# List batches of 9, 9, 12 and 6 tiles, with their work spread over other iterations of the main loop

## What is computed

```python
q = x @ Wq.T + bq; k = key @ Wk.T + bk; v = value @ Wv.T + bv
scores = (q @ k.T) / sqrt(4096)
adj_scores = scores * adj
adj_scores = where(abs(adj_scores) < 1e-05, -1e9, adj_scores)
prob = softmax(adj_scores, axis=-1)
y = (prob @ v) @ Wm.T + bm
out = layernorm(x + y)
```

## Time and profile before

| | |
|---|---|
| median of 3 runs | 504.44 us (504.05 to 504.83) |
| the profiled execution | 507.02 us, span 505.2 us |
| granted TensorE clock, mean | 0.971 |
| PE busy | 455.5 us, 90% |
| VectorE (DVE) busy | 329.7 us, 65% |
| Pool (POOL) busy | 258.7 us, 51% |
| ScalarE (ACT) busy | 215.2 us, 43% |
| DMA | 119.73 MB, mean 237 GB/s |

### The profile page before, as it was taken

The page is one execution under the profiler, slowest core; times in us unless marked ns, Lnnn a source line. Parts: engine busy times, 40 slices in busy tenths (PEclk is TensorE's granted clock), DMA queues, the critical chain, the costliest instruction groups (busy, mean ns, idle before and its releaser), DMA issues.

```text
span 505.2 us, 5747 instructions
## 1 busy us (share of the span) xinstructions
PE 455.5 (90%) x1556; PEld 250.0 (49%) x1556; DVE 329.7 (65%) x905; ACT 215.2 (43%) x471; POOL 258.7 (51%) x258
## 2 busy tenths in 40 slices
PE   6999999999998398999998878589999989999981
PEld 2444444444443145665655545356666555665551
DVE  0155444599239914889899889976875864654774
ACT  1223322233331124434653444425656536556574
POOL 2100001201860017788787888617777757777730
PEclk9999999999999879999998999979999989999998
DMA  8999998799999958999999999818677665765743
GB/s 312 357 212 247 276 286 209 134 269 290 258 301 273 271 140 261 242 275 271 238 330 296 261 304 294 255 49 254 187 226 242 213 198 172 221 188 168 227 151 123
DMA packets 42037, 119.73 MB, mean 237 GB/s; under 512 B 7109, under 2 KB 11973, under 8 KB 40978
## 3 DMA queue, kind: packets, MB, share of 16 engines
q0 software_dynamic: 19008, 70.59, 56.6%
q1 hardware_dynamic: 15842, 28.91, 16.2%
q10 hardware_dynamic: 7152, 19.83, 10.7%
HBM read 140.61 MB, written 17.83 MB: 314 GB/s over the span
## 4 chain that ended last, share of the span: by engine, by line
PE 53%; DVE 30%; ACT 7%; issue 5%; DMA 4%; POOL 1%; DVEq 0%; POOLq 0%; ACTq 0%
PE bank L548 13%; PE bank L539 10%; PE bank L681 7%; PE bank L661 7%; PE bank L641 4%; DVE big L981 3%; PE bank L579 3%; DMA big<-adj_tiles 3%; PE bank L593 3%; DVE big L1020 3%; DVE big L1018 2%; DVE y_buf L1183 2%; DVE big L983 2%; DVE big L1051 2%; DVE big L1048 2%
## 5 line engine op out<-in xcount | busy, mean ns | idle before, releaser
L548 PE MATMUL bank<-big,M 128*128 128x456 f32 x288 | 121.6, 548 | 1.8 <-DMA big<-xT 1.8
L539 PE MATMUL bank<-y_buf,big 128*128 128x512 f32 x256 | 111.2, 594 | 0.0
L428 POOL DMA_INDIRECT key_g<-key,index x72 | 77.0, 1070 | 43.0 <-DVE index L1062 22.0
L439 POOL DMA_INDIRECT v_g<-table,index x72 | 78.4, 1089 | 36.5 <-issue 18.3
L450 POOL DMA_INDIRECT adj_g<-adj_cols,index x72 | 75.5, 1048 | 21.9 <-issue 21.6
L419 POOL DMA_DIRECT2D big<-adj_tiles x36 | 20.6, 574 | 122.5 <-PE bank L539 69.8
L981 DVE TENSOR_TENSOR big<-big 128x1824 bf16<-128x1824 bf16 x36 | 39.6, 1101 | 60.4 <-DMA big<-adj_tiles 60.4
L539 PEld LDWEIGHTS bank<-y_buf,big 128*128 128x128 f32 x256 | 48.2, 190 | 59.6 <-issue 59.6
L681 PE MATMUL bank<-v_g,probT 128*114 128x512 f32 x140 | 70.5, 628 | 0.0
L661 PE MATMUL bank<-keyT,qT 128*114 128x256 f32 x288 | 68.5, 381 | 0.8 <-ACT keyT L854 0.5
L548 PEld LDWEIGHTS bank<-big,M 128*128 128x128 f32 x288 | 49.6, 190 | 33.1 <-issue 33.1
(11 more groups left out here) (115 smaller groups left out, 535.6 us busy)
## 6 DMA issues: line engine op xcount, KB each, us to landing
big<-adj_tiles POOLq DMA_DIRECT2D x36, 912.0 KB, 11.0
x_buf<-x SPq DMA_DIRECT2D x36, 256.0 KB, 4.9
out<-y_buf SPq DMA_DIRECT2D x35, 256.0 KB, 2.7
big<-valueT ACTq DMA_DIRECT2D x8, 1024.0 KB, 11.4
big<-xT SPq DMA_DIRECT2D x7, 912.0 KB, 8.6
table<-qT ACTq DMA_DIRECT2D x5, 1024.0 KB, 20.1
table<-y_buf ACTq DMA_DIRECT2D x3, 1024.0 KB, 23.8
big<-xT ACTq DMA_DIRECT2D x2, 912.0 KB, 20.2
```

Of the source, the lines that this page charges most:

```text
L428: pool.indirect_dma_start(key_g[:, b, c, :], None, key, bass.IndirectOffsetOnAxis(index[:, t, c:c + 1], 0), bounds_check=N - 1, oob_is_err ...
L439: pool.indirect_dma_start(v_g[:, b, c, :], None, table, bass.IndirectOffsetOnAxis(index[:, t, c:c + 1], 0), bounds_check=N - 1, oob_is_err ...
L539: mm = nc.tensor.matmul(bank[4 + t % 2][:, :], col_buf[nb % 2][:, d, k * P:(k + 1) * P], G[:, d, :], start=(d == 0), stop=(d == DC - 1))
L548: mm = nc.tensor.matmul(ps[:, 0:QR], M[:, d, a * P:(a + 1) * P], col_buf[nb % 2][:, d, 0:QR], start=(d == 0), stop=(d == DC - 1))
```

## The change

The tiles are dealt to four batches of 9, 9, 12 and 6 (`BATCH`, `START`); the third has 96 cells, the fourth 48. The operands of the list work are cut to the batch's partitions; `cell_count` and `cell_need` are cleared at the start, since not every partition is written now.

Tiles 20 to 29 are reduced in iterations 0 to 9 and tiles 30 to 35 in 15 to 20. Pool's loads move with them (they follow `trees_of(i + 3)`). Batch 2 has its steps in iterations 10 to 15, batch 3 in 21 to 26. There are six steps instead of eight: step 0 has numbering, count and a pass, steps 1 and 2 two passes each, step 3 the last pass, the bits and the first two pairs of the shift, step 4 the other six pairs, step 5 the index. Numbering moves behind the weights and statistics, and `add_x` stays ahead of the weights in step 0 too. `COUNTS` goes from 25 to 27.

On PE the lists' products (`lists`, `sum_counts`, `spread_slots` and the two of the overflow test) move from behind the scores to just ahead of the transposes of the probabilities.

Ahead of the loop `value_sums` moves from behind tile 19 to between batch 1's last pass and its bits, and `index_slots(1)` behind `key_bias(0)`. Pool waits for an index at tiles 0, 9, 18 and 30 instead of 0, 9, 18 and 27.

The diff, cut to its core:

```diff
-BT = 9
-LB = T // BT
+BATCH = (9, 9, 12, 6)
+START = (0, 9, 18, 30)
+LB = len(BATCH)
+BT = max(BATCH)
...
-        TREES = [[t] for t in range(FIRST, T)]
-        LIST_AT = {2: 8, 3: 17}
-        COUNTS = 25
+        TREES = {i: [FIRST + i] for i in range(10)} | {i: [FIRST + i - 5] for i in range(15, 21)}
+        LIST_AT = {2: 10, 3: 21}
+        COUNTS = 27
...
-                if at <= i <= at + PASSES + 1:
+                if at <= i <= at + 5:
...
-                if t % BT == 0:
-                    pool.wait_ge(index_ready, (t // BT + 1) * (2 * CH))
+                if t in START:
+                    pool.wait_ge(index_ready, (START.index(t) + 1) * (2 * CH))
...
             def lists(b):
-                pe.wait_ge(any_sb, (b + 1) * BT)
+                n = BATCH[b] * G8
+                pe.wait_ge(any_sb, START[b] + BATCH[b])
                 if b > 2:
                     pe.wait_ge(index_ready, b * (2 * CH))
                 for k in range(K4):
-                    mm = nc.tensor.matmul(list_bank(b)[0:CELLS, k * P:(k + 1) * P],
-                                          any_[:, k, b * BT:(b + 1) * BT, :].rearrange("p t g -> p (t g)"),
+                    mm = nc.tensor.matmul(list_bank(b)[0:n, k * P:(k + 1) * P],
+                                          any_[:, k, START[b]:START[b] + BATCH[b], :].rearrange("p t g -> p (t g)"),
                                           ident16[:, :], start=True, stop=True)
                 mm.then_inc(list_ps, 1)
...
-                if step == 0:
-                    lists(b)
-                if step == 1:
-                    sum_counts(b)
-                if step == PASSES + 1:
-                    spread_slots(b)
-                if i == COUNTS + 1:
-                    pe.wait_ge(lead_sb, 2)
-                    for k in range(2):
-                        mm = nc.tensor.matmul(bank[6][0:1, k * P:k * P + CELLS], lead[:, k:k + 1], ident[0:CELLS, 0:CELLS],
-                                              start=True, stop=True)
-                    mm.then_inc(lead_ps, 1)
                 if i >= 1:
                     values(i - 1)
                 if i + 1 < T:
@@ -718,6 +711,18 @@
                     if i == 0:
                         pe.wait_ge(bits_sb, 2 * 2)
                     project(u, bank[7], 0, 1)
+                if step == 0:
+                    lists(b)
+                if step == 1:
+                    sum_counts(b)
+                if step == 5:
+                    spread_slots(b)
+                if i == COUNTS + 1:
+                    pe.wait_ge(lead_sb, 2)
+                    for k in range(2):
+                        mm = nc.tensor.matmul(bank[6][0:1, k * P:k * P + CELLS], lead[:, k:k + 1], ident[0:CELLS, 0:CELLS],
+                                              start=True, stop=True)
+                    mm.then_inc(lead_ps, 1)
...
+            nc.vector.memset(cell_count[:, :], 0.0).then_inc(filled, 1)
+            nc.vector.memset(cell_need[:, :], 0.0).then_inc(filled, 1)
...
-            def shift_lists(b):
-
+            def shift_lists(b, first, last):
+
+                c = cells_of(b)
                 dve.wait_ge(took, (b + 1) * (2 * PASSES))
-                wide = LIST
-                for k in range(SHIFTS):
+                for k in range(first, last):
                     by = 1 << k
+                    wide = min(LIST + by - 1, ROOM)
...
-                if t == 2 * BT - 1:
+                if t == START[2] - 1:
                     number(1)
                     count(1)
                     for k in range(PASSES):
                         take_8(1, k)
+                    value_sums()
                     shift_bits(1)
-                    shift_lists(1)
-            value_sums()
-            index_slots(1)
+                    shift_lists(1, 0, SHIFTS)
             dve.wait_ge(prep_sb, 2 * DC + 2)
             key_bias(0)
+            index_slots(1)
...
-                if step == 0:
-                    number(b)
-                elif 1 <= i <= LAST_QUERY:
+                if 1 <= i <= LAST_QUERY:
                     add_x(i - 1)
                 if i < T:
                     weigh(i)
-                if i >= 1 and (step == 0 or i > LAST_QUERY):
+                if i > LAST_QUERY:
                     add_x(i - 1)
                 if 1 <= i < T:
                     statistics(i - 1)
                 if i == T:
                     last_statistics(T - 1)
-                if step == PASSES + 1:
+                if step == 5:
                     index_slots(b)
                 for t in trees_of(i):
                     reduce_tile(t)
                 if step == 0:
+                    number(b)
                     count(b)
-                if step is not None and step < PASSES:
-                    take_8(b, step)
-                if step == PASSES:
+                    take_8(b, 0)
+                if step in (1, 2):
+                    take_8(b, 2 * step - 1)
+                    take_8(b, 2 * step)
+                if step == 3:
+                    take_8(b, PASSES - 1)
                     shift_bits(b)
-                    shift_lists(b)
+                    shift_lists(b, 0, 2)
+                if step == 4:
+                    shift_lists(b, 2, SHIFTS)
```

More of the change, by code:

```diff
@@ L1004, in count @@
                     dve.wait_ge(took, b * (2 * PASSES))
-                nc.vector.tensor_scalar(lw, left[:, b, :], 0.0, 0.0, ALU.is_gt, ALU.add,
-                                        accum_out=cell_count[:, b:b + 1]).then_inc(counted, 1)
+                nc.vector.tensor_scalar(lw[c, :], left[c, b, :], 0.0, 0.0, ALU.is_gt, ALU.add,
+                                        accum_out=cell_count[c, b:b + 1]).then_inc(counted, 1)
                 for k in range(2):
-                    nc.vector.memset(dense[k], 0.0).then_inc(cleared, 1)
+                    nc.vector.memset(dense[k][c, :], 0.0).then_inc(cleared, 1)
                 dve.wait_ge(counted, b + 1)
@@ L1012, in take_8 @@
             def take_8(b, i):
+                c = cells_of(b)
                 k = b * (2 * PASSES) + 2 * i
-                src = left[:, b, :] if i == 0 else lw
+                src = left[c, b, :] if i == 0 else lw[c, :]
                 if i:
                     dve.wait_ge(took, k)
-                row = dense[0][:, 8 * i:8 * i + 8]
+                row = dense[0][c, 8 * i:8 * i + 8]
                 nc.vector.max(row, src).then_inc(took, 1)
                 dve.wait_ge(took, k + 1)
-                nc.vector.match_replace(lw, row, src, 0.0).then_inc(took, 1)
+                nc.vector.match_replace(lw[c, :], row, src, 0.0).then_inc(took, 1)
@@ L1022, in shift_bits @@
             def shift_bits(b):
+                c = cells_of(b)
                 dve.wait_ge(sums_ps, b + 1)
-                first = list_bank(b)[0:CELLS, 64:65]
+                first = list_bank(b)[c, 64:65]
                 if b >= 1:
                     dve.wait_ge(shifted, b * (2 * SHIFTS))
-                nc.vector.tensor_scalar(first_slot[:, :], first, float(SLOTS - 1), None, ALU.min).then_inc(first_sb, 1)
-                nc.vector.tensor_tensor(cell_need[:, b:b + 1], first, cell_count[:, b:b + 1], ALU.add).then_inc(need_sb, 1)
+                nc.vector.tensor_scalar(first_slot[c, :], first, float(SLOTS - 1), None, ALU.min).then_inc(first_sb, 1)
@@ L1030, in shift_bits @@
+                nc.vector.tensor_tensor(cell_need[c, b:b + 1], first, cell_count[c, b:b + 1], ALU.add).then_inc(need_sb, 1)
                 dve.wait_ge(first_sb, b + 1)
-                nc.vector.tensor_tensor(digit[:, :], first_slot[:, 0:1].broadcast_to([CELLS, SHIFTS]),
-                                        cst[0:CELLS, C_BIT:C_BIT + SHIFTS].bitcast(I32), ALU.bitwise_and).then_inc(digit_sb, 1)
+                nc.vector.tensor_tensor(digit[c, :], first_slot[c, 0:1].broadcast_to([BATCH[b] * G8, SHIFTS]),
+                                        cst[c, C_BIT:C_BIT + SHIFTS].bitcast(I32), ALU.bitwise_and).then_inc(digit_sb, 1)
@@ L1279, in _ @@
+                            nc.vector.tensor_tensor(g_spread[0:n, c, :].rearrange("p (g s) -> p g s", g=G8),
+                                                    group_mask[0:n], slots[0:n, c * SPC:(c + 1) * SPC].unsqueeze(1)
+                                                    .broadcast_to([n, G8, SPC]), ALU.mult).then_inc(g_spread_sb, 1)
                         wait_apart(dve, g_spread_ps, r * (LB * CH) + (b + 1) * CH)
-                        tiles = slice(b * BT, (b + 1) * BT)
+                        tiles = slice(START[b], START[b] + BATCH[b])
```

60 lines of the change are left out of this document (32 added, 28 removed).

## The result

The changed kernel takes 487.0 us (median of 4 runs, 485.82 to 491.21) where the kernel before, beside it, takes 504.5 (4 runs, 504.05 to 504.83): a ratio of 0.9641, 95% interval 0.9591 to 0.9691. Forecast were 487.4. The profiled execution took 485.82 us, its span 484.0, at a mean granted clock of 0.984.

What follows compares the result with a forecast made beforehand. DVE was taken to bound iterations with trees or list work, PE the others, Pool a hardly slacker second chain. DVE's chain allowed 18.6 + 0.5 = 19.1 us, Pool's 17.5; 17.0 taken from 504.44 gave 487.4, range 483 to 494.

Steps and rivals of the forecast that it cites:

- DVE's pieces: Loop: busy times of tree, passes, shifts and index added per iteration; 8 to 15 fall from 83.48 to 66.7 us.
- Iterations 16 to 20: Five iterations with late trees, one with square roots: 40.5 us, 0.7 more than before.
- the 4 that would have counted against it: Sign of failure: PE waits for key_g in iterations 18 to 22 by more than 4 us in all.
- Pool's chain: Pool's 31 gather rounds, tiles 4 to 35: 264.7 us plus 1 of index wait; at most 17.5 us won.
- The page on the port: Pool's rounds 12 to 14, load but no tree: page says no gain, row up to 0.8 us each; sum made without it.
- The head: Ahead of the loop, value sums moved earlier: 0.5 us won, with 5.0 and -1.5 as ends.
- the worse end: Ahead of the loop: SP's load shares the DMA engines, value gathers begin 1.5 us later, PE ends 1.1 later.
- The products' place: PE's list products moved ahead of the probability transposes: costs nothing, bound 0.5 us for each of six sets, 3.
- DMA saturation: Rival: loads of rounds 12 to 17 saturate the DMA engines, 8.2 us given back, 495.6; chance 0.17.
- The good rival: Head gains fully, 2 to 5 us, and rounds 12 to 14 up to 2.4: 483; chance 0.12.
- Products: Rival: products ahead of the transposes hold PE at steps 0, 1 and 5; at 3.64 us each, 509; chance 0.03.
- no change: Rival: Pool at 9.4 us a round was the bound all along, index waits only move: 504; chance 0.02.

## Why the prediction was right, step by step

- **DVE's pieces hold.** Iterations 8 to 15: forecast 66.7, measured 67.40, of which 1.95 are waits for keys (0.40 and 1.55). Iteration 10 was put at 8.44 (8.82), 14 at 8.74 (8.63), 15 at 8.29 (8.27). 21 to 30: forecast 82.9, measured 80.90; the largest miss in it is iteration 26, put at 8.3 and 6.81 long, then 24 and 25 (7.94 and 8.62 for 8.41 and 9.1), against 0.75 too little for 21 and 22. The experiment with the trees left in place shows that this separation is most of the gain.
- **Iterations 16 to 20** were put at 40.5 and last 42.96. The 2.5 more lie in 19 and 20, where PE waits for keys: 1.26 + 1.29 + 1.39 = 3.94 from 18 to 20. That is above the 1 to 3 us forecast, and only just under the 4 that would have counted against it.
- **Pool's chain sets the pace only as far as tile 21.** The sum was made on its last gather, that of tile 35, and there the step is wrong in its mechanism: behind tile 21 PE waits for no gather, and PE, busy for 80.44 of 80.90 us in iterations 21 to 30, sets the end. That the sum came out near is luck in part, since Pool's light rounds (8.05) and PE's iterations (8.09) there are of one length. Pool's rounds from tile 4 to tile 35 took 460.60 - 199.39 = 261.21, forecast 265.7. The six first rounds are 9.22 each (9.36), the 19 light ones 8.05 to 8.07 (8.02), the index wait nothing (1). The mis-sized term is the six loads that moved: rounds 12 to 14 are (320.83 - 295.05) / 3 = 8.59 each, rounds 15 to 17 (347.89 - 320.83) / 3 = 9.02, where the sum had 9.36 for all six. The gather of tile 35 is used 4.22 after its issue (forecast 3.6).
- **The page on the port.** I had set the rule of the Trainium skill's "SBUF — State Buffer", under "Who interferes with whom" (the trees' tensor_tensor doesn't take what descriptor writing needs, so rounds 12 to 14 gain nothing), against a row that let them gain up to 0.8 each. They came 0.77 under the 9.36 taken, so the row was right, and the trace shows by what. A gather whose issue falls on a tree's first step (L989, 1.09 long) is held until 0.8 to 0.9 behind the step's end; the issue of a plain load isn't:

```profile
226.03 1.09 DVE L989 TENSOR_TENSOR big<-big 128x1824 bf16<-128x1824 bf16 x1
226.23 1.79 POOL L430 DMA_INDIRECT key_g<-key,index  x1 [0.30 <-issue]
...
317.84 1.09 DVE L989 TENSOR_TENSOR big<-big 128x1824 bf16<-128x1824 bf16 x1
318.11 0.61 POOL L421 DMA_DIRECT2D big<-adj_tiles  x1
```

In the changed kernel's loop nine gathers begin 0.1 to 0.4 behind the start of such a step. They take 1.63 to 1.84, where the median of all is 1.00; in the kernel before it is eight, with 1.63 to 1.83. A gather that begins ahead of the step isn't held (342.06, 0.12 ahead: 0.96). The rounds with a load follow it. With no gather held they are 8.39 to 8.66 long (five rounds, 12 and 13 among them, which have no tree beside them, but also 17, which has one). With one held they are 9.28 to 9.55 (five), with two 10.11. Round 14 lies between with 8.88: the tree of iteration 15 already holds one of its gathers for 1.50. What of the issue is held isn't shown.

- **The head.** L629 starts at 167.67 without a wait, the next wait is the transfer, the projection behind it runs at the lower level, the keys' first transposes are at 186.75, where 188 to 191 was forecast: about 1 us of it because what stands ahead already ran that much sooner in this execution (161.46, where the earlier trace rows has 162.47). Value gathers 0.25 later, within the +1.2 to -1.5 given. The rule of the Trainium skill's "DMA: Bandwidth & Descriptors", under "Queues, rings and completion order" (a DMA engine goes round its queues, a packet at a time), called for the worse end: SP's load, issued sooner, takes its share at once. The store's 28.5 instead of 26.4 agrees in kind; its end, at 157.38 + 28.5 = 185.9, lies between the ends. The block of xT doesn't show it: it took 23.6 instead of 24.4. For the loop's start the 0.5 us taken was far too small, since it comes 4.2 sooner (190.60 for 194.80). For the total it was near: in the changed kernel the head is worth nothing that the runs tell, though alone, in the kernel that DVE still bounds, it is worth 2.7.
- **The products' place** was costed at nothing, with 3 as a bound; the experiment shows 0.9 in its trace, at iteration 26, and nothing that the totals tell.
- **The rivals.** DMA saturation: the share is 1.01 in iterations 16 to 20, as it says, but 15 to 20 take 364.84 - 313.61 = 51.2, not 57.0 (48.8 in my sum): 2.4 of its 8.2. The good rival had its second half right (lighter rounds, 2.3 of its 2.4) and its first wrong in effect. Products and no change fall.
- **The total was closer than its parts.** Between the two profiled executions the span is 21.2 shorter, 4.2 more than forecast. By stretches the gain is 4.2 ahead of the loop (0.5 taken), 16.1 in iterations 8 to 15 (16.8), -3.2 in 16 to 20 (-0.7), 4.5 in 21 to 30 (2.5) and -0.4 in the rest; forecast were 19.1 in all, taken down to 17.0 for Pool. Between the medians it is 17.5, because the profiled execution before lay 2.6 above its median and the one after 1.2 below. That 487.4 met 487.0 so closely is luck: the trace's 4.2 too much and the 3.8 by which the two executions stood apart from their medians cancel. A sum made from one execution can't be held to better than that.

## What to carry to other kernels

When two kinds of work of one engine are each small enough to fit beside the rest, but not both, put them into different iterations: that, and not the order within an iteration, was most of the gain here. Before counting such a gain, add up the engine that only issues transfers, round by round and with its waits taken out: it was busy half the time, and yet its gathers held PE up as far as tile 21, and made the head's 4 us worthless. Look also for where such a chain stops to bind; here it was PE from there on. And look for what lengthens its issues: a gather that fell on a tree's first step took some 0.7 us longer, so DVE's trees cost Pool too. Where a wait is removed, look for the transfer that is late next, and for what shares the DMA engines with it.

## What the runs showed of the hardware

- An idle stretch costs PE twice: the same eight products took 3.30 us after a wait of 2.19, at a granted share of 1.00 (with the load of tile 22 late), and 5.49 after one of 5.86, at a mean share of 0.60 (changed kernel).
- How long a gather takes to land goes with the load issued ahead of it. In the kernel before, the key gathers of tiles 4 to 16, each issued right behind a load, landed after 6.9 to 12.6, those of tiles 17 to 35, with none, after 3.4 to 6.7. In the changed kernel that of tile 35, with none, took 3.4, those of tiles 10 and 21, behind a load, 10.26 and 10.56. How busy the DMA engines are differs as well.
- A gather that Pool issues 0.1 to 0.4 us behind the start of DVE's 1.09 us bf16 tensor_tensor step is held: 1.63 to 1.84 us instead of 1.00. The issue of a plain load beside the same step takes its usual 0.61.
- Leaving one 912 KB load out from among others moved the landing of a block of xT by 5.9 us (176.81 and 182.72), and the first value gather, which waits for the last store of the table, by 7.4 (180.39 and 187.82).
- The same kernel took 487.0 us on one chip and 536 on two others, with stalls of 3 to 12 us at changing places that no row explains, and the ratio of the two kernels went from 0.964 to between 0.985 and 0.989. A gain measured on one chip need not have the same size on another.
